# Keeping the residual in the output: accumulating stores, layer-norm sums by transfer, and a lead-in in 256-token blocks

## The chip, the cores and the metric

The kernel runs on one core of a Trainium2 chip. Its engines are TensorE (PE in the profile, its weight loads PEld), VectorE (DVE), ScalarE (ACT), GpSimd (POOL) and SyncE (SP), which here only issues transfers. The metric is the device time of one execution in microseconds; lower is better. Before the change it is 1020.83 us, the median of 3 runs (1020.34 to 1025.84).

## The reference, cut to what matters

Two batches of 1024 tokens with 2048 features. A quantized product with a context matrix is added to x, then a linear layer with a routed low-rank term is added to that:

```python
q1 = fake_quant(layernorm(x), x1_scale, x1_zp)      # (2, 1024, 2048)
q2 = fake_quant(ctx, x2_scale, x2_zp)               # (2, 2048, 2048)
x2 = x + q1 @ q2
xf = layernorm(x2)
probs = softmax(xf @ W_router.T)                    # 8 experts, the best 2, renormalized to w
h = einsum('td,erd->ter', xf, lora_A)               # rank 16
lora = einsum('ter,eor,te->to', h, lora_B, w) * 2
out = x2 + xf @ W_base.T + b_base + lora
```

## The kernel before, in words

Everything is held transposed, features on partitions and tokens along the row. An output row is 128 features by 1024 tokens of float32, 512 KB; there are NT = 16 of them in each of NB = 2 batches.

First product. A batch of x is loaded in 8 tiles of 128 tokens (`xn_load`), VectorE takes statistics (L333), GpSimd five tiny steps (L336 to L340), ScalarE quantizes to bytes (L348), TensorE transposes the bytes (L361), and VectorE or ScalarE writes them back as bf16 (L376, L378). A context row is loaded, quantized (L400) and converted to bf16 by VectorE, ScalarE or GpSimd (`ctx_conv`, L410 and L412). `gemm1` (L455) multiplies it into two PSUM banks; `evac1` (L473) scales the sum and adds x. That is an output row of x2. `keep` stores it to the DRAM tensor `kept`. Rows of batch 0 stay in SBUF (`XA`), those of batch 1 pass through two stage buffers.

In the lead-in the first three output rows are made together, while the tiles of batch 0 come in: the first 512 tokens of each row, then 256, then 256.

Layer norm over x2. The sum over the 16 rows is gathered row by row (`add0`, `add1`, L508), a matmul with a constant spreads the mean (`ones`, L485), VectorE subtracts it (`centre0` L520, `centre1` L549), ScalarE squares (L526, L556), and VectorE or GpSimd sum the squares (`square0` L533; `centre1` L557). `var_a` (L569 to L578) and `var_b` turn the sum into the scale. For batch 1 the rows are read back from `kept` (`tile_load`), and the centred ones go through DRAM and come back (`ln_load`).

Second product. The 2048 by 2048 matrix product of a batch is done as 8 blocks of 256 features. A block takes 7 products instead of 8, from sums and differences of quarters of the operand (`y_operands`, L616 to L618) and of the weights (`w_sum` L810), each value split in two f16 halves: the high half on ScalarE (`w_hi` L826), the low one as a difference on VectorE or GpSimd (`w_lo` L831, with `la`, `lt`, `lb` in `y_operands` at L617). `product` (L865 to L867) and `tail` (low-rank term, L886 to L888) fill three of six PSUM banks; the next block uses the other three. A weight scale is found by `w_norm`, with one small step on GpSimd (L709). `lora_h` is at L968 to L970.

Around the change. For each block, `ob_load` brings two output rows of `kept` back into a buffer, `ob_bias` (L905, ScalarE) adds the bias, and `post` adds scaled PSUM banks to the buffer (L915, VectorE, six times a block), apart from product 0, which is copied to a second bank (L929 ScalarE, L931 VectorE). `store` writes the buffer to the output. TensorE waits for some of these evacuations: product 3 for that of product 0, product 4 for that of 2, product 5 for that of 1, product 6 for that of 4.

Each engine has its own queue (`Line`), served strictly in order, with semaphore waits ahead of each instruction. The order is made by a plan: `at(t, f, ...)` gives each step a planned time, steps are sorted by it, and the table `V` holds offsets and the choice of engine ("a", "d", "p" for ScalarE, VectorE, GpSimd). SyncE's transfers (`Loads`) are sorted by the same times. The planned times only fix an order. A slow path for other zero points is skipped: each engine loads a flag (set by VectorE, L240) and branches, before the first instruction of the planned work (`both`, L1298; L1296 loads the flag).

Of the kernel before, what the change touches and what calls it, by code (L numbers as in the profile page):

```python
# [4 lines left out]
ACT = mybir.ActivationFunctionType  # L5
# [11 lines left out]
NT = 16  # L17
# [8 lines left out]
    "ctx_load": (-21.4, -16.79), "x_load": (-8.52, -2.7), "ctx_quant": (-10.38, -11.98), "ctx_conv": (-8.14, -5.53),  # L26
    "quant_on": "aaaaaaaaaaaaaaaaaaaaaaaaaaaaaaaa", "conv_on": "ddpappdpapaapdaadaadaaaaaapapdap", "evac_a": (9.81, 3.95),
    "evac_b": (5.43, 6.35), "keep": (20.76, 3.77), "ln1_step": 10.32, "xn_load": -13.2, "ln1_stats": -2.38,
    "ln1_quant": 3.24, "ln1_turn": 13.26, "ln1_back": 15.39, "back_on": "dddaaadd", "add0": 9.92, "mean": 3.5,
    "centre": 2.69, "centre_step": 2.3, "square": 2.58, "square_on": "dpppdppppppdpppd", "add1": 8.92, "sq_end": 6.2,  # L30
    "var_a": 7.58, "var_b": 12.06, "early": (8.48, 4.32, 10.86, 17.6, 0.72, 14.76, -4.36), "ops0": -54.07,
    "ops0_step": 9.0, "ops0_in": (3.06, 3.83, 1.69, 0.31, 2.05, -0.86, 3.32, 3.28), "lt_on": "pdpppdpddddddddd",
    "add1_on": "ppdddpddpppppppd", "sq1_on": "pdpppdpdppdddpdp", "lb_on": "dddddddddddddddd", "y_on": "ad",
    "post": ((-0.42, -0.62, 0.55, 0.9, 4.11, 0.34, 0.76), (1.78, 2.26, 0.1, 1.17, 1.58, 0.41, 1.32)),
    "la_on": "dpdddpdddpdpdpdp", "first_raw": -11.49, "first_ring": -0.52, "raw0": 8.82, "norm1": 40.01,
    "norm1_step": 6.14, "tile_load": -5.9, "cd_store": 1.64, "yd_store": 1.76, "var1": 7.44, "ops1": 11.14,
    "ops1_step": 19.58, "ln_load": 2.27, "ops1_in": (10.61, 1.45, 3.66, 2.38, 5.98, 7.8, 9.35, 3.61), "start": 32.08,
    "pair": 39.04, "a_load": 8.72, "a_prep": 18.75,
    "router": ((3.6, -4.9, 12.48, 1.98, 4.87, 8.83, 9.75, 24.24, 22.77), (1.64, -15.29, 12.16, 0.96, 2.87, 21.06, 13.87, 14.95, 23.73)),
    "w_load": (-31.54, -27.81, -27.96, -19.33), "b_load": -27.3,  # L40
    "w_norm": ((-20.87, -23.36, -22.49, -22.9), (-14.88, -21.6, -16.62, -15.26)),
    "w_scaled": ((-16.21, -11.48, -15.49, -9.58), (-12.98, -14.22, -14.22, -2.35), (-22.26, -18.56, -24.17, -27.91), (-18.78, -10.27, -4.7, -8.89)),
    "w_b": (11.13, -5.59, -17.37, -1.76),
    "w_op": ((-11.4, -3.44, -3.15, -9.51, -7.61, 8.03, 4.96), (-10.2, -7.05, 0.4, -4.29, 5.17, 2.6, 1.94), (-13.14, 16.12, 2.8, -20.29, 13.81, 2.35, 14.01), (6.02, -16.16, 16.7, 8.23, -0.09, 12.25, -1.78)),
    "w_sum": (8.38, 1.9, 0.3, -25.41, 1.16, 1.16, -3.26), "lo_on": ("pdpddpp", "pdppddp"), "ob_load": (-6.91, -12.75),
    "ob_bias": (-0.26, 1.49),
# [3 lines left out]
class Line:  # L50
# [6 lines left out]
    def do(self, waits, emit):  # L57
        self.work.append((waits, emit))
        self.done += 1
        return (self.sem, self.done)  # L60

    def run(self, eng, first=0, last=None):
        for waits, emit in self.work[first:last]:
# [46 lines left out]
def xattn_lora_ffn(nc, xn, xT, cT, qp, wT, bias, aT, rT, bT, outT, kept, maps):  # L110
# [107 lines left out]
    sl_yl = slots("sl_yl", 7)  # L218
# [322 lines left out]
    def tile_load(i):  # L541
        s = i % 2
        tile_in[i] = sp.do(tile_free[s] + [keep_out[NT + i]], sl_tb[s], tb[s], kept[1, i])
        tile_free[s] = None
# [826 lines left out]
```

## Time and profile before

| | |
|---|---|
| time, median of 3 runs | 1020.83 us (1020.34 to 1025.84) |
| the profiled execution | 1021.56 us, of which its span is 1018.8 us |
| mean granted clock of TensorE | 0.983 of full speed |
| busy: PE, DVE, ACT, POOL | 939.1, 631.1, 505.3, 303.2 us |
| moved by transfers | 211.74 MB, mean 208 GB/s |

The span runs from the first to the last instruction; the rest of the execution's own time lies around it. Busy time counts instructions that compute, not waits and not the issuing of transfers. A name such as "DVE S L810" is the engine, the tile written and the line of the kernel. A group of instructions shows busy time, the mean duration in ns and the idle time ahead with what ended it.

### The profile page before, as it was taken

How to read it: one execution, taken by the hardware profiler on the slowest of the kernel's cores; microseconds unless marked ns; L12 is line 12 of the kernel's file. 1: busy time of each engine (PE TensorE's matmuls, PEld its weight loads, DVE VectorE, ACT ScalarE, POOL GpSimd, SP SyncE). 2: the span in 40 equal slices, each digit the busy share in tenths (PEclk: the TensorE clock that was granted, in tenths of full speed). 3: DMA queues.
4: the chain of work that ended last, by engine and by line, in shares of the span. 5: the costliest groups of instructions: out<-in, count | busy, mean ns of one | idle time of the engine just before them, and what ended most of it. 6: DMA issues, size and time to landing. Idle time of an engine off the chain costs nothing. (4 is left out here: it accounts for less than half of the span.)

```text
span 1018.8 us, 12800 instructions
## 1 busy us (share of the span) xinstructions
PE 939.1 (92%) x4448; PEld 433.8 (43%) x4470; DVE 631.1 (62%) x760; ACT 505.3 (50%) x473; POOL 303.2 (30%) x217
## 2 busy tenths in 40 slices
PE   1899999998778898999899899998999999999998
PEld 0454444443334444344344344443444444444443
DVE  5788677989988585757869787315643253252251
ACT  4765676965556465555556565304443333334330
POOL 3333204836532053333314222102122122121220
PEclk9999999999999899999999999999999999999999
DMA  9789996876630557756675685991332332322311
GB/s 349 313 325 399 394 334 247 292 262 209 256 140 22 212 199 254 257 210 225 213 263 194 217 285 181 363 397 67 124 141 77 124 123 95 124 103 114 125 42 41
DMA packets 65044, 211.74 MB, mean 208 GB/s; under 512 B 6096, under 2 KB 22608, under 8 KB 56400
## 3 DMA queue, kind: packets, MB, share of 16 engines
q1 hardware_dynamic: 64976, 210.86, 56.5%
q8 instruction: 39, 0.64, 0.2%
q14 instruction: 29, 0.24, 0.1%
HBM read 154.22 MB, written 56.62 MB: 207 GB/s over the span
## 5 line engine op out<-in xcount | busy, mean ns | idle before, releaser
L831 POOL TENSOR_TENSOR Q<-S,Q 128x1024 f16<-128x1024 f32 x43 | 95.3, 2223 | 228.0 <-ACT Q L826 202.3
L826 ACT ACTIVATE Q<-S 128x1024 f16<-128x1024 f32 x74 | 77.2, 1049 | 114.5 <-DVE S L810 113.6
L867 PE MATMUL PS<-XA,Q 128*128 128x512 f16 x336 | 127.3, 379 | 0.0
L865 PE MATMUL PS<-XA,Q 128*128 128x512 f16 x336 | 127.3, 379 | 0.0
L866 PE MATMUL PS<-XA,Q 128*128 128x512 f16 x336 | 127.3, 379 | 0.0
L455 PE MATMUL PS<-Q,S 128*128 128x512 bf16 x501 | 114.5, 386 | 13.3 <-POOL S L412 6.0
L793 ACT ACTIVATE S<-S,WC 128x1024 f32<-128x1024 f32 x64 | 70.1, 1139 | 98.9 <-DMA S<-in_wT_dram 70.3
L455 PE MATMUL PS<-EX,S 128*128 128x512 bf16 (+1 forms) x502 | 106.4, 369 | 4.8 <-DVE st L333 2.0
L915 DVE SCALAR_TENSOR_TENSOR Q<-PS,WC,Q 128x512 f32<-128x512 f32 x72 | 53.6, 747 | 90.2 <-PE PS L888 60.7
L865 PE MATMUL PS<-EX,Q 128*128 128x512 f16 x256 | 98.6, 385 | 11.7 <-DVE S L915 7.1
L867 PE MATMUL PS<-EX,Q 128*128 128x512 f16 x256 | 98.5, 385 | 0.0
L866 PE MATMUL PS<-EX,Q 128*128 128x512 f16 x256 | 98.3, 384 | 0.0
L810 DVE TENSOR_TENSOR S<-S 128x1024 f32<-128x1024 f32 x64 | 93.7, 1466 | 5.2 <-ACT S L793 3.9
L831 POOL TENSOR_TENSOR S<-S 128x1024 f16<-128x1024 f32 x21 | 46.8, 2231 | 162.1 <-ACT S L826 156.8
L455 PEld LDWEIGHTS PS<-Q,S 128*128 128x128 bf16 x512 | 50.4, 100 | 76.6 <-POOL S L412 6.7
L455 PEld LDWEIGHTS PS<-EX,S 128*128 128x128 bf16 x512 | 50.2, 99 | 57.4 <-DVE EX L378 3.7
L915 DVE SCALAR_TENSOR_TENSOR S<-PS,WC,S 128x512 f32<-128x512 f32 x24 | 17.9, 745 | 83.0 <-PE PS L888 82.8
L865 PE MATMUL PS<-XA,S 128*128 128x512 f16 x176 | 66.7, 379 | 0.0
L867 PE MATMUL PS<-XA,S 128*128 128x512 f16 x176 | 66.7, 379 | 0.0
L866 PE MATMUL PS<-XA,S 128*128 128x512 f16 x176 | 66.7, 379 | 0.0
L826 ACT ACTIVATE S<-S 128x1024 f16<-128x1024 f32 x38 | 39.6, 1048 | 54.1 <-DVE S L810 54.0
L400 ACT ACTIVATE S<-S,cst 128x2048 uint8<-128x2048 f32 x30 | 62.5, 2082 | 4.5 <-DMA S<-in_cT_dram 4.5
(217 smaller groups left out, 1617.9 us busy)
## 6 DMA issues: line engine op xcount, KB each, us to landing
S<-in_cT_dram SPq DMA_DIRECT2D x32, 1024.0 KB, 8.0
S<-in_wT_dram SPq DMA_DIRECT2D x32, 1024.0 KB, 5.4
EX<-in_xn_dram SPq DMA_DIRECT2D x24, 512.0 KB, 7.5
Q<-kept_dram SPq DMA_DIRECT2D x24, 512.0 KB, 6.5
S<-kept_dram SPq DMA_DIRECT2D x24, 512.0 KB, 4.6
out_dram<-Q SPq DMA_DIRECT2D x24, 512.0 KB, 2.9
yops_dram<-S SPq DMA_DIRECT2D x48, 256.0 KB, 3.3
XA<-in_xT_dram SPq DMA_DIRECT2D x16, 512.0 KB, 9.0
```

Of the source, the lines that this page charges most:

```text
L400: f = lambda e: e.activation(u8b[u], ctx_f[s], ACT.Identity, bias=z2, scale=inv2)
L455: ins = e.matmul(bank(a)[:, t0 % 512:t0 % 512 + t1 - t0], q2[q][:, 128 * k:128 * (k + 1)], q1T[b][:, k, t0:t1], start=(k == 0), stop=(k == ...
L793: scaled_w[i, q] = [act.do([raw_in[q // 2]] + w_scale[i % 8][0], lambda e, v=v: e.activation(v, v, ACT.Copy, bias=0.0, scale=c[:, 4:5]))]
L810: sub = lambda w, dst, x, y, op=ALU.subtract: [dve.do(w, lambda e: e.tensor_tensor(dst, x, y, op))]
L826: tok["hi", n] = s, free, src, act.do(w + free, lambda e: e.activation(ring[s][:, 0:1024], src, ACT.Copy, bias=0.0, scale=1.0))
L831: l = line.do([h] + free, lambda e: e.tensor_tensor(ring[s][:, 1024:2048], src, ring[s][:, 0:1024], ALU.subtract))
L865: e.matmul(bank(bk), wh[:, c], yh(op, k), start=(fresh and k == 0), stop=False, skip_group_check=not fresh)
L866: e.matmul(bank(bk), wh[:, c], yl(op, k), start=False, stop=False, skip_group_check=not fresh)
L867: ins = e.matmul(bank(bk), wl[:, c], yh(op, k), start=False, stop=(read and k == 7), skip_group_check=not fresh)
L915: ob_ready[i, h] = [dve.do(done + ob_ready[i, h] + w_scale[i % 8][2], lambda e: e.scalar_tensor_tensor(dst, src, kk, dst, op0=ALU.mult, op ...
```

## The change

1. `kept` is no longer used: `keep` stores rows of x2 into the output tensor, and what read `kept` reads the output.
2. For all blocks but the last, `ob_load` and `ob_bias` go. The first evacuation into each half of a buffer writes bias + scaled product (`first`, on ScalarE or VectorE by `first_on`; batch 0: one VectorE, three ScalarE; batch 1: four VectorE), and `store` becomes a transfer issued by GpSimd that adds the buffer to the output. The last block works as before, but stores each 128 x 512 quarter by itself once finished.
3. Six additions of layer-norm sums ("m" in `add1_on` at 9, 14, 15; in `sq1_on` at 1, 3, 15) become accumulating transfers from SBUF to SBUF issued by GpSimd. The "m" in `square_on` at 1 is at a place that isn't used.
4. The lead-in's products run in blocks of 256 tokens, in an order of their own, and VectorE's branch moves behind the statistics of the first two tiles. The lead-in's engines and times come from `V`.
5. `centre0` also waits for the row's `keep`. SyncE's last waits include the `keep` and last stores.
6. Most numbers in `V` and many engine choices are new, among them: conversions of context rows 1 and 2 on GpSimd, of the last row (31) on ScalarE (was GpSimd); the bank copy of batch 1 on ScalarE (was VectorE).

```diff
+    def move(self, waits, slot, dst, src):
+        self.work.append((waits, lambda e: e.dma_start(dst, src, accum_op=ALU.add), slot.sem))
+        return slot.next()
...
-            emit(eng).then_inc(self.sem, 1)
+            if moved is None:
+                emit(eng).then_inc(self.sem, 1)
+            else:
+                emit(eng).then_inc(moved, 16)
...
-        keep_out[g] = sp.do(w + both_halves(g), sl_keep[g % 4], kept[g // NT, g % NT], xt(g))
+        keep_out[g] = sp.do(w + both_halves(g), sl_keep[g % 4], outT[g // NT, g % NT], xt(g))
...
+    def add_to(on, w, acc, v, slot=sl_add):
+        if on == "m":
+            return pool.move(w, slot, acc, v)
+        return lines[on].do(w, lambda e: e.tensor_tensor(acc, acc, v, ALU.add))
...
+        def first(h, dst, src, on):
+            col = bo[:, 2 * (i % 8) + h:2 * (i % 8) + h + 1]
+            w = done + ob_free[(2 * i + h) % 4] + w_scale[i % 8][2] + [once["bo"]]
+            if on == "a":
+                e = act.do(w, lambda e: e.activation(dst, src, ACT.Identity, bias=col, scale=kk))
+            else:
+                e = dve.do(w, lambda e: e.tensor_scalar(dst, src, kk, col, op0=ALU.mult, op1=ALU.add))
...
-        elif n in (1, 4):
-            e = acc(1, L[:, t1], bank(bk))
...
+            e = acc(h, v, bank(bk)) if n in (4, 5) or i == LAST else first(h, v, bank(bk), V["first_on"][i // 8][{1: 0, 2: 1, 3: 2, 6: 3}[n]])
+            if i == LAST and n > 2:
+                last_store(h, 1 if n in (4, 5) else 0, v, e)
...
-        ob_free[d] = [sp.do(ob_ready[i, h], sl_out[d], outT[b, o], ob[d])]
+        ob_free[d] = [pool.move(ob_ready[i, h] + [keep_out[NT * b + o]], sl_out[d], outT[b, o], ob[d])]
...
+    at(V["l_stats"][1] + 0.01, split_dve)
...
+    for n, (g, t0, t1) in enumerate(((0, 0, 256), (1, 0, 256), (0, 256, 512), (1, 256, 512), (2, 0, 256), (2, 256, 512),
+                                     (0, 512, 768), (1, 512, 768), (2, 512, 768), (0, 768, 1024), (1, 768, 1024), (2, 768, 1024))):
+        at(V["l_gemm"][n], gemm1, g, t0, t1, 0, 16)
```

## Rows read from the trace of the kernel before

**Rows 1.** The page: span, and TensorE's busy time.
```profile
span 1018.8 us, 12800 instructions
...
PE 939.1 (92%) x4448; PEld 433.8 (43%) x4470; DVE 631.1 (62%) x760; ACT 505.3 (50%) x473; POOL 303.2 (30%) x217
```

**Rows 2.** Busy time by stretches: length, then engines as named, clock, DMA share, GB/s.
```profile
0.00:60.00 60.00, 31.95 (x187) 20.21 (x191) 42.58 (x70) 35.83 (x20) 19.07 (x54) 1.00 0.83 317
...
150.00:350.00 200.00, 173.79 (x821) 78.69 (x830) 165.95 (x202) 125.82 (x117) 91.40 (x41) 0.96 0.58 208
...
400.00:650.00 250.00, 232.69 (x1054) 104.56 (x1053) 184.06 (x214) 143.28 (x161) 80.49 (x39) 0.97 0.66 234
...
750.00:1019.00 269.00, 264.89 (x1228) 119.84 (x1226) 95.56 (x100) 87.23 (x87) 53.58 (x25) 1.00 0.26 101
```

**Rows 3.** Waits of TensorE in 400 to 650 (total, times, longest); its timeline.
```profile
PE PS L865 <- DVE S L915: 11.1, 3, 4.1
...
496.15 0.38 PE L865 MATMUL PS<-EX,Q 128*128 128x512 f16 x1 [4.14 <-DVE S L915]
```

**Rows 4.** Timelines of VectorE and GpSimd: start, us, instruction, idle time ahead.
```profile
488.81 1.22 DVE L616 TENSOR_TENSOR S<-S,PS 128x1024 f32<-128x1024 f32 x1 [1.06 <-DMA S<-centred_dram]
...
492.19 3.15 DVE L810 TENSOR_TENSOR S<-S 128x1024 f32<-128x1024 f32 x1
...
492.14 2.12 POOL L831 TENSOR_TENSOR S<-S 128x1024 f16<-128x1024 f32 x1 [6.42 <-ACT S L826]
...
535.99 1.22 DVE L810 TENSOR_TENSOR S<-S 128x1024 f32<-128x1024 f32 x1
```

**Rows 5.** Groups by shape, whole span: busy us, mean ns, idle before.
```profile
L915 DVE SCALAR_TENSOR_TENSOR Q<-PS,WC,Q 128x512 f32<-128x512 f32 x72 | 53.6, 747 | 90.2 <-PE PS L888 60.7 <-PE PS L867 28.0
...
L905 ACT ACTIVATE Q<-Q,bo 128x1024 f32<-128x1024 f32 x24 | 27.0, 1134 | 0.0
...
L929 ACT ACTIVATE PS<-PS 128x512 f32<-128x512 f32 x8 | 4.6, 580 | 0.0
```

**Rows 6.** Waits in 400 to 650 of SyncE's queue and of GpSimd.
```profile
SPq L102 <- DVE Q L915: 64.3, 14, 12.7
...
POOL Q L831 <- ACT Q L826: 59.4, 12, 6.5
```

**Rows 7.** The page's DMA issues: count, KB each, median us to landing.
```profile
out_dram<-Q SPq DMA_DIRECT2D x24, 512.0 KB, 2.9
...
kept_dram<-XA SPq DMA_DIRECT2D x16, 512.0 KB, 9.1
```

**Rows 8.** Timelines around the last output row of the first product, and low-rank product.
```profile
275.47 8.37 PE L455 MATMUL PS<-Q,S 128*128 128x512 bf16 x31 [6.02 <-POOL S L412]
...
270.59 2.96 POOL L617 TENSOR_TENSOR EX<-S,EX 128x1024 f16<-128x1024 f32 x1 [5.12 <-DVE PS L617]
...
262.22 2.08 ACT L400 ACTIVATE S<-S,cst 128x2048 uint8<-128x2048 f32 x1
...
311.05 0.38 PE L968 MATMUL PS<-XA,S 128*128 128x512 f16 x1 [1.53 <-DVE XA L617]
```

**Rows 9.** Timelines: last addition of batch 1's squares, and the variance's matmul.
```profile
449.46 2.37 POOL L557 TENSOR_TENSOR S<-S 128x1024 f32<-128x1024 f32 x1 [4.79 <-ACT S L556]
...
454.63 1.84 PE L569 MATMUL PS<-mean_w,S 128*128 128x1 f32 x16
```

**Rows 10.** VectorE's first work, and the first four half tiles, issue to landing.
```profile
3.07 0.16 DVE L240 TENSOR_TENSOR flag<-rr 128x1 int32<-128x1 f32 x1
9.72 2.47 DVE L333 BATCH_NORM_STATS2 st<-EX 128x6 f32<-128x512 f32 x4 [6.49 <-issue]
...
L102 SPq DMA_DIRECT2D EX<-in_xn_dram x4: 420/432/432, 1.2 to 2.6; - x4
...
DMA to landing us min/median/max: 4.2/5.8/8.9
```

**Rows 11.** Timeline of SyncE: the last store's issue.
```profile
1015.71 0.33 SPq L102 DMA_DIRECT2D out_dram<-S  x1
```

More of the change, by code:

```diff
@@ L57, in do @@
     def do(self, waits, emit):
-        self.work.append((waits, emit))
+        self.work.append((waits, emit, None))
         self.done += 1
         return (self.sem, self.done)
+    def move(self, waits, slot, dst, src):
+        self.work.append((waits, lambda e: e.dma_start(dst, src, accum_op=ALU.add), slot.sem))
+        return slot.next()
     def run(self, eng, first=0, last=None):
-        for waits, emit in self.work[first:last]:
+        for waits, emit, moved in self.work[first:last]:
             for sem, value in waits:
                 eng.wait_ge(sem, value)
-            emit(eng).then_inc(self.sem, 1)
+            if moved is None:
+                emit(eng).then_inc(self.sem, 1)
+            else:
+                emit(eng).then_inc(moved, 16)
 class Slot:
@@ L507, in add1 @@
         else:
-            sums[1] = [lines[V["add1_on"][nt]].do(sums[1] + both_halves(NT + nt), lambda e: e.tensor_tensor(acc1, acc1, t, ALU.add))]
+            sums[1] = [add_to(V["add1_on"][nt], sums[1] + both_halves(NT + nt), acc1, t)]
         stage_free[nt % 2] = stage_free[nt % 2] + sums[1]
@@ L556, in centre1 @@
             sq = act.do([y] + sq_free[s], lambda e: e.activation(sq1[s], v, ACT.Square))
-            sums[1] = [lines[V["sq1_on"][i]].do(sums[1] + [sq], lambda e: e.tensor_tensor(acc1, acc1, sq1[s], ALU.add))]
+            sums[1] = [add_to(V["sq1_on"][i], sums[1] + [sq], acc1, sq1[s])]
             sq_free[s] = list(sums[1])
@@ L1106, in split_here, with split_dve @@
         sp.split = len(sp.work)
+    def split_dve():
+        assert sorted(front) == [(0, 0), (0, 1)]
+        dve.split = len(dve.work)
     P = Plan()
@@ L1275, in xattn_lora_ffn @@
         for h in range(2):
-            at(us(t + V["ob_load"][h]), ob_load, i, h)
-            at(us(t + V["ob_bias"][h]), ob_bias, i, h)
+            if i == LAST:
+                at(us(t + V["ob_load"][h]), ob_load, i, h)
+                at(us(t + V["ob_bias"][h]), ob_bias, i, h)
+            else:
+                at(us(t + V["store"][h]), store, i, h)
         when = [5.12 * n for n in range(6)] + [33.3]
@@ L1312, in _ @@
             sp.run(eng, sp.split, None, case)
-            for s in sl_out:
+            for s in sl_keep + sl_out + sl_last:
                 eng.wait_ge(s.sem, 16 * s.n)
```

105 lines of the change are left out of this document (53 added, 52 removed).

## The prediction

> **What bounds the kernel now.** First the page's busy shares: TensorE is busy for 939.1 of 1018.8 us [rows 1], so I ask where the other 80 us are and which engine makes them. The table by stretches [rows 2] answers: 28.0 us idle in 0 to 60 (the lead-in), 26.2 in 150 to 350 (first layer norm of the output, operands of batch 0, low-rank term), 17.3 in 400 to 650 (blocks of batch 0 with the second layer norm beside them) and 4.1 behind 750, nearly all of it the tail. The column PEclk adds the time that TensorE ran at the lower of its two levels, 1.2 GHz instead of 2.4: 0.97 over 250 us is 7.5 us of lost work, 0.96 over 200 us is 8. What a change can win lies in three places, then: about 28, 34 and 25 us. From 750 to the tail TensorE never waits and nothing can be won.
>
> Next, who ends these waits. In 400 to 650 it is VectorE's evacuation L915: 11.1 us in three waits, the longest 4.14 us [rows 3]. That one, read on VectorE and GpSimd, is a queue and not one slow instruction [rows 4]: the subtraction L616 waits 1.06 us for a reloaded centred row, a sum L810 takes 3.15 us instead of the 1.22 of its neighbour because a GpSimd subtraction that began 0.05 us earlier runs for 2.12 us, and only then comes the L915 on which TensorE waits. So this stage is bound by the length of VectorE's queue.
>
> **Part 1: the residual stays in the output.** In each of the 16 blocks but the last, two loads of 512 KB, two ScalarE bias additions of 1.134 us and the read-modify-write form of four of the six evacuations go. In batch 0 three of the four become ScalarE activations (0.58 us by the nearest row, the copy L929) and one stays on VectorE. VectorE loses 3 x 0.747 = 2.2 us a block, 18 us over eight blocks; ScalarE loses 2 x 1.134 and gains 3 x 0.58, so 0.5 us less [rows 5]. In batch 1 VectorE sheds eight bank copies, where TensorE has no idle time: worth nothing.
>
> The stores leave SyncE's queue. Today they hold it: 64.3 us in 14 waits in 400 to 650 alone [rows 6], with the loads of weights and centred rows behind them. They go to GpSimd's queue, which is busy 80 of 250 us there, as 30 accumulating transfers, and the weights' low halves (L831) and the small step L709 then stand behind them. GpSimd now comes to an L831 5.0 us before its input is there (59.4 us over 12 waits) [rows 6]. The stores are placed at 33.0 and 42.7 us of a block whose last evacuations come at about 32.6 and 38.5, so they should find their rows ready.
>
> No row shows an accumulating transfer or one issued by GpSimd. For the landing, the nearest rows are 512 KB in 2.9 us (store) and in 9.1 us (store under load) [rows 7]; a buffer is wanted again two blocks, some 78 us, later, so either hides. For GpSimd's own time I take 1 us, near SyncE's 0.33 us an issue [rows 11], with 0.33 and 9.1 as ends. Even 9.1 fits the idle share (2 x 9.1 in a block of 39 us), but a subtraction queued behind it comes late; that is the fourth case below. The Trainium skill (DMA: Bandwidth & Descriptors, section "Anatomy of one DMA") gives 2.0 us plus bytes over 436 GB/s for such a transfer, 3.2 us here as an estimate; nothing here shows it, and the sum below would be 1 us lower by it, since the wait of part 3 would vanish.
>
> What this wins: of the 4.14 us stall, 1.06 (the reload, queued behind stores) and 0.75 (an evacuation ahead) go by rows 4 and 5, that is 1.8 or 44%. The GpSimd overlap stays, and the evacuation that TensorE waits for there is a read-modify-write that stays on VectorE. I apply a third, not 44%, to the stage's 25 us, because every instruction's place is re-planned and new meetings will form: **-8 us**, ends -25 (all of it) and +8 (as much lost as I count won).
>
> **Part 2: layer-norm sums by transfer and new placing, 60 to 350.** Three adds of the batch-1 sum leave GpSimd (2) and VectorE (1). The largest stall of this stage is 6.02 us before the last output row of the first product: its conversion sat on GpSimd, in order behind a subtraction that ended at 273.55, though its quantized input was ready on ScalarE at 264.30 [rows 8]. That conversion is now ScalarE's, so this stall goes, 6.0 us, with 1.7 for one stretch at the lower clock. But most is given back at once: what TensorE does next ends on operands that VectorE makes without a pause, and it waited for them at 311.05. There VectorE sheds one add (1.2) and one low-half subtraction (1.2); the earlier product does not speed that chain. I take **-3 us**, ends -7.7 (nothing given back) and +5 (four conversions more on VectorE in the first half of the rows, 1.2 us each, should they land in its full stretch).
>
> **Part 3: the last add of the batch-1 squares** becomes a transfer and gates the variance's matmul. Now it starts at 449.46 and takes 2.37 us on GpSimd; the matmul comes at 454.63 with no wait [rows 9]. With a landing of 2.9 to 9.1 us the sum is there at 452.4 to 458.6, so the wait is 0 to 3.9 us: **+1 us**. The same kind of step earlier in the chain has 6 us between rows and hides.
>
> **Part 4: lead-in.** VectorE takes the general-case branch behind two tiles' statistics and no longer ahead of them. Now it sets the flag at 3.07 and starts statistics only at 9.72, 6.5 us idle, while the first half tile had landed at 1.2 + 4.2 = 5.4 and, by the median of the four, the second near 7 [rows 10]. If the branch costs little when taken later, 9.7 - 5.4 = 4.3 us are won. If it costs its 6.5 us again: tile 1's last half lands at 2.6 + 8.9 = 11.5, its statistics end near 13.0, and VectorE is back at 19.5 with 5.4 us of work done (two tiles of four statistics, 2.47 us, and their aggregation), where today it has done 9.8 by then. That is 4.4 late, less two passes of 1.2 us net that leave it, so 2.0 late. Blocks of 256 tokens let TensorE begin with tiles 0 and 1 alone, but the conversion of the first context row now stands behind tiles 2 and 3 on VectorE, so it begins no sooner, and the last tile comes at about the same time either way. I take **0**, between ends of -4.3 and +2 and nearer the second: three microseconds of the idle time lie behind the landings, so the branch itself is dear.
>
> **Tail.** Last store issued 1015.71, span end 1018.8 [rows 11, 1]: 3.1 us for 512 KB. It becomes quarters of 256 KB: **-0.3**, ends 0 and -1.5.
>
> **Sum.** 0 - 8 - 3 + 1 - 0.3 = -10.3. The profiled execution took 1021.56 us for a span of 1018.8, so 1011.3 for one like it; that execution lies 0.73 above the median of 1020.83, so 1010.5. I say **1011**.
>
> **Rivals.**
> *Everything in 400 to 650 goes.* 184 us of VectorE work in 250 leave room, and 13 go. Against it: the GpSimd overlap that made half of the long stall is untouched. -25 - 3 - 0.3 + 1 gives 994; with half of the gain beyond mine, 1001.
> *Given back: no change.* GpSimd's issues hold the port or buffers that VectorE's two-input sums need, as its subtraction did for 1.93 us in rows 4. Sixteen issues in batch 0 at 1.93 us are 31 us of VectorE time at worst, 18 less what evacuations freed: the stage keeps its 25 us, and 1020.8 - 3 + 1 - 0.3 + 1.7 is 1020. For it: VectorE is 74% busy there. Against: no row says that an issue does what a 1024-wide subtraction does. The Trainium skill's page SBUF — State Buffer ("Who interferes with whom") has descriptor writes by GpSimd and VectorE's two-port modes exclude each other; by that rule it is the transfer that waits, and the trace shows the exclusion only between compute instructions.
> *Slower: the stores block GpSimd's queue.* Place: a store waits, or is being issued, while a low half (L831) for TensorE's next product stands behind it. It decides from the point where wait and issue together exceed the 5.0 us by which GpSimd is now ahead [rows 6]. Price: a stall like the longest now, 4.14 us, with 1.7 at the lower clock, once in three of the eight blocks of batch 0 is +17.5, and no gain of 8: 1020.8 - 2.3 + 17.5 = 1036. For it: in-order queues did just this with the 6.02 us conversion. Against: GpSimd idles two thirds of that stage.
>
> **How the numbers follow.** Forecast (1003 to 1016) 0.48, no change 0.23, slower 0.20, far faster 0.09. A measurement here can tell 0.5%, about 5 us. So faster (under 1015.7) 0.56, the same 0.23, slower (over 1025.9) 0.21. The range of the forecast alone is 1003 to 1017; to hold 8 in 10 it must take in no change and the nearer part of the slower case: **999 to 1031**.
>
> **What would show it.** Right: in the table by stretches the idle time and PEclk of 400 to 650 improve to some 17 us together; no wait over 4 us for L915; no wait near the last output row of the first product, but a longer one for VectorE's operands behind it; SyncE no longer waits for L915. Part 4: a gap of about 6 us on VectorE behind tile 1. Wrong: waits of TensorE for GpSimd's L831, GpSimd waiting for L915 with L831 behind it, VectorE sums of 2 us or more beside issues, or a new wait over 4 us at the variance matmul.

## The result, and the profile after

| | before | changed |
|---|---|---|
| median (range, executions) | 1021.43 us (1019.02 to 1025.84, 20) | 1018.19 us (1010.24 to 1022.36, 20) |
| ratio, 95% interval | | 0.9963 [0.9946, 0.998] |
| measured again beside experiments | 1021.26; 1021.95 us | 1014.45, ratio 0.993 [0.9912, 0.9948]; 1016.51, ratio 0.9956 [0.9936, 0.9976] |

The forecast was 1011, a gain of 10. The first measurement gives a gain of 3.2 us; the three ratios average 0.995, a gain of 5 us: right in direction and inside the range, but half the size or less. The changed kernel's executions spread over 12 us where those of before spread over 7, so below I also compare stages of the profiled executions. The repeats are e5 (1014.45) and e15 (1016.51). Of e5 I had expected 1016 to 1019 if the kernel itself varies and some 1012 if the first chip was unlucky; it came between.

The changed kernel's profiled execution took 1018.26 us. Its page: span and busy times, the DMA queues (packets, MB, share of 16 engines' span) and GpSimd's stores (KB each, us to landing).

```profile
span 1016.5 us, 12911 instructions
...
PE 938.8 (92%) x4518; PEld 438.7 (43%) x4518; DVE 613.5 (60%) x708; ACT 495.4 (49%) x475; POOL 357.3 (35%) x267
...
q1 hardware_dynamic: 56624, 179.40, 48.6%
q0 software_dynamic: 5184, 18.88, 11.1%
...
out_dram<-Q POOLq DMA_DIRECT2D x23, 512.0 KB, 5.5
```

VectorE does 17.6 us less and GpSimd 54.1 more than in [rows 1], of which 31.7 are its 36 issues (of GpSimd, unlike SyncE, the page counts issues as busy time). The new queue q0 is GpSimd's: 18.88 MB in 11.1% of the transfer engines' time, where q1 moves 9.5 times as much in 4.4 times the time. That disproportion is the key to this case. (5.5 us is the landing of the 23 stores from buffers called Q; the seven from buffers called S took 7.9.) Next the table by stretches, columns as in [rows 2]:

```profile
0.00:60.00 60.00, 31.56 (x236) 25.32 (x237) 37.98 (x62) 37.71 (x21) 15.85 (x50) 1.00 0.85 319
...
150.00:350.00 200.00, 177.86 (x837) 79.87 (x835) 161.36 (x194) 120.96 (x111) 93.78 (x45) 0.94 0.60 208
...
400.00:650.00 250.00, 228.99 (x1047) 103.38 (x1046) 171.37 (x194) 144.04 (x166) 92.19 (x52) 0.98 0.67 202
...
750.00:1017.00 267.00, 263.09 (x1219) 119.11 (x1217) 102.39 (x79) 77.95 (x82) 93.22 (x51) 1.00 0.32 84
```

In 400 to 650 VectorE lost 12.7 of its 184.1 us of work, as forecast, and yet TensorE's idle time did not fall: 21.0 us here, 18.2 and 17.1 in the profiles of e5 and e15, against 17.3 before. The waits of that stretch, of TensorE, VectorE, GpSimd and SyncE, say where to look; they answer to [rows 3, 6]:

```profile
POOL Q L854 <- ACT Q L849: 60.8, 12, 11.5
...
DVE S L639 <- DMA S<-centred_dram: 20.3, 11, 3.4
...
PE PS L888 <- DVE S L938: 10.4, 3, 5.4
```
```profile
SPq L117 <- ACT S L641: 71.4, 24, 10.0
SPq L115 <- DMA centred_dram<-S: 32.4, 6, 9.0
```

The same two waits in the kernel before, VectorE's for the reload and SyncE's for the landing of a centred row that it has stored:

```profile
DVE S L616 <- DMA S<-centred_dram: 3.4, 4, 1.1
```
```profile
SPq L100 <- DMA centred_dram<-S: 20.1, 5, 9.7
```

(L639, L854, L888, L938 and L641 were L616, L831, L865, L915 and L618 before.) VectorE waits 20.3 us for reloaded centred rows, six times as long as before (15.2 and 14.4 in e5 and e15). SyncE no longer waits for evacuations, as forecast, but it is held as long by the next step in its order: the operand quarters of L641, 71.4 us (66.9 and 68.8 in e5 and e15) against the 64.3 for L915, and by the centred rows' own stores, 32.4 us against 20.1. One stall read on VectorE, then on TensorE:

```profile
577.10 2.43 DVE L639 TENSOR_TENSOR S<-S,PS 128x1024 f32<-128x1024 f32 x2 [3.40 <-DMA S<-centred_dram]
579.63 1.42 DVE L640 TENSOR_TENSOR S<-S 128x512 f32<-128x512 f32 x2
580.97 1.22 DVE L833 TENSOR_TENSOR S<-S 128x1024 f32<-128x1024 f32 x1
582.10 0.74 DVE L938 SCALAR_TENSOR_TENSOR S<-PS,WC,S 128x512 f32<-128x512 f32 x1
```
```profile
583.00 0.58 PE L888 MATMUL PS<-EX,S 128*128 128x512 f16 x1 [3.87 <-DVE S L938]
```

This is the queue of [rows 4] again, with 3.40 us of waiting at its head instead of 1.06. TensorE's wait (3.87) is about that wait plus a short step, so by these rows, though no run shows it for this one stall, the evacuation would have come nearly in time without it.

I cut the execution at TensorE's last low-rank product (`tail`) of block 0 and of block 7. "Reload wait" is VectorE's for `centred_dram` in 400 to 650.

| kernel (profiled execution, us) | to block 0 | blocks 1 to 7 | rest | reload wait |
|---|---|---|---|---|
| before | 369.4 | 301.6 | 347.8 | 3.4 |
| changed, three profiles (first, e5, e15) | 369.3, 368.9, 369.3 | 303.2, 301.7, 300.8 | 344.0, 344.0, 345.6 | 20.3, 15.2, 14.4 |
| forecast of the difference | -3 | -8 +1 | -0.3 | |

So blocks 1 to 7 won nothing, the way to block 0 won nothing, and what was won in the profiles lies behind block 7, where I had said next to nothing could be. Of the kernel before there is one profile only. The kernel of e7 (below), which differs from it in the lead-in alone, took 371.5, 303.1 and 346.2 us: differences of up to 2 us between single profiles can be chance.

### The profile page after: what moved, and what is told of

Read it like the earlier page. It is cut to its first block, busy times and chain, and to the rows that moved or that the text cites. A ratio compares the mean times of both kernels' runs of the same rounds, so it can differ in the third digit from the quotient of the medians.

```text
span 1016.5 us, 12911 instructions
## 1 busy us (share of the span) xinstructions
PE 938.8 (92%) x4518; PEld 438.7 (43%) x4518; DVE 613.5 (60%) x708; ACT 495.4 (49%) x475; POOL 357.3 (35%) x267
## 3 DMA queue, kind: packets, MB, share of 16 engines
q0 software_dynamic: 5184, 18.88, 11.1%
## 4 chain that ended last, share of the span: by engine, by line
PE 46%; DVE 9%; DMA 9%; issue 4%; ACT 2%; POOL 2%; SPq 0%; DVEq 0%; ACTq 0%; POOLq 0%
PE PS L888 13%; PE PS L890 12%; PE PS L889 12%; DMA S<-centred_dram 4%; DVE S L640 4%; DMA yops_dram<-S 2%; DMA S<-in_wT_dram 2%; DVE S L639 1%; PE PS L1002 1%; PE PS L1003 1%; PE PS L1004 1%; PE PS L909 1%; PE PS L911 1%; PE PS L910 1%; PE PS L1045 1%
## 5 line engine op out<-in xcount | busy, mean ns | idle before, releaser
L854 POOL TENSOR_TENSOR Q<-S,Q 128x1024 f16<-128x1024 f32 x54 | 117.8, 2189 | 124.3 <-ACT Q L849 118.1
L888 PE MATMUL PS<-XA,Q 128*128 128x512 f16 x336 | 127.3, 379 | 1.3 <-POOL Q L854 1.3
L833 DVE TENSOR_TENSOR S<-S 128x1024 f32<-128x1024 f32 x64 | 102.0, 1594 | 33.2 <-POOL Q L854 20.9
L472 PE MATMUL PS<-Q,S 128*128 128x512 bf16 x512 | 116.7, 390 | 5.3 <-POOL S L429 3.0
L888 PE MATMUL PS<-EX,Q 128*128 128x512 f16 x256 | 98.5, 385 | 13.5 <-DVE S L938 6.5
L854 POOL TENSOR_TENSOR S<-S 128x1024 f16<-128x1024 f32 x26 | 58.9, 2270 | 56.2 <-ACT S L849 56.2
L472 PEld LDWEIGHTS PS<-EX,S 128*128 128x128 bf16 x544 | 53.8, 99 | 50.6 <-DVE st L350 0.9
L523 POOL TENSOR_TENSOR S<-S 128x1024 f32<-128x1024 f32 x25 | 63.0, 2529 | 26.9 <-ACT S L549 13.2
L71 POOL DMA_DIRECT2D out_dram<-Q x23 | 20.2, 879 | 140.8 <-DVE Q L947 105.9
L888 PE MATMUL PS<-XA,S 128*128 128x512 f16 x176 | 66.7, 379 | 0.0
L640 DVE TENSOR_TENSOR S<-S 128x512 f32<-128x512 f32 (+2 forms) x68 | 64.5, 969 | 2.3
```

Source lines behind the costliest of these rows:

```text
L71: self.work.append((waits, lambda e: e.dma_start(dst, src, accum_op=ALU.add), slot.sem))
L472: ins = e.matmul(bank(a)[:, t0 % 512:t0 % 512 + t1 - t0], q2[q][:, 128 * k:128 * (k + 1)], q1T[b][:, k, t0:t1], start=(k == 0), stop=(k == ...
L523: return lines[on].do(w, lambda e: e.tensor_tensor(acc, acc, v, ALU.add))
L640: diff = lambda dst, x, y, w, line=dve: line.do(w, lambda e: e.tensor_tensor(dst, x, y, ALU.subtract))
L833: sub = lambda w, dst, x, y, op=ALU.subtract: [dve.do(w, lambda e: e.tensor_tensor(dst, x, y, op))]
L854: l = line.do([h] + free, lambda e: e.tensor_tensor(ring[s][:, 1024:2048], src, ring[s][:, 0:1024], ALU.subtract))
```

## Experiments

**One, two and no accumulating packets.** In 400 to 650 q0 of the changed kernel moved 6.80 MB in 16.1% of 16 x 250 us, which is 388 ns for each 4 KB on one engine. The first run (e3) makes GpSimd's 30 stores plain, which leaves the residual out of all blocks but the last. The six sums by transfer still accumulate.

```diff
-        ob_free[d] = [pool.move(ob_ready[i, h] + [keep_out[NT * b + o]], sl_out[d], outT[b, o], ob[d])]
+        pool.work.append((ob_ready[i, h] + [keep_out[NT * b + o]], lambda e: e.dma_start(outT[b, o], ob[d]), sl_out[d].sem))
+        ob_free[d] = [sl_out[d].next()]
```

> The changed kernel, whose 30 stores by GpSimd are plain and not accumulating (the residual is left out of all but the last block of the output). Theory A: nothing that TensorE waits for changes, 1016 to 1020, VectorE's waits for the reload stay near 20 us. Rival B: the operands' stores land in 3.3 us again and not 4.0, the waits halve and the time is 1010 to 1013.

It took 1012.48 us (ratio 0.9921 [0.9894, 0.9947]) and the reload wait was 8.1 us: the rival's time and its halved wait, though the operands' stores landed in 3.7 us and not in 3.3. Since the changed kernel's own measurements differed by 3.7 us, this was repeated on one chip with the changed kernel and with two that store each buffer twice, the second time into the scratch tensor:

```diff
+        ob_free[d].append(pool.move([], sl_dup[d], kept[b, o], ob[d]))
```

In the second of them (e14) the additional transfer is plain:

```diff
+        pool.work.append(([], lambda e: e.dma_start(kept[b, o], ob[d]), sl_dup[d].sem))
+        ob_free[d].append(sl_dup[d].next())
```

> The changed kernel, and behind each of GpSimd's 30 accumulating stores a second one of the same buffer into the scratch tensor, so the accumulating packets are doubled (16 more of 512 KB in batch 0, 14 in batch 1); its output is the same. Theory (packets of 389 ns hold the transfer engines, the reload of centred rows comes late, VectorE's evacuation with it): 4 to 8 us over the changed kernel beside it, waits for the reload in 400 to 650 of 25 us or more (20.3 and 15.2 in the two profiles of the changed kernel), and 2 us or more above the next kernel. Rival (the packets are hidden and the lost microseconds are the new order's): within 2 us of the changed kernel beside it.

> The changed kernel, and behind each of GpSimd's 30 accumulating stores a second, plain one of the same buffer into the scratch tensor: the same additional issues on GpSimd (0.88 us each) and the same bytes from SBUF, but packets of 181 ns by the plain stores seen so far. Theory (the time of the packets is the price): 1 to 4 us over the changed kernel and 2 us or more below the kernel with doubled accumulating stores. Rival 1 (GpSimd's issue is the price): the same as that kernel within 1 us. Rival 2 (hidden): within 1 us of the changed kernel.

> The changed kernel as it is, on the chip of the two runs with doubled stores, since its own two measurements (1018.19 and 1014.45 us) differ by more than the effect in question. Theory: 1014 to 1018, below both of the others. Rival (hidden): the three lie within 2 us.

> The changed kernel with GpSimd's stores as plain transfers, residual left out of all blocks but the last (1012.48 us when run beside a changed kernel of another job), now on the chip of the changed kernel and of the doubled stores, so that none, one and two accumulating packets of each row stand on one scale. Theory: 3 to 6 us under the changed kernel beside it, and as far below it as the doubled one lies above. Rival (hidden): within 2 us of it.

| stores of each row | median us | ratio | blocks 1 to 7 | reload wait |
|---|---|---|---|---|
| plain (e16) | 1011.58 | 0.9914 [0.9882, 0.9946] | 297.2 | 7.4 |
| accumulating, as changed (e15) | 1016.51 | 0.9956 [0.9936, 0.9976] | 300.8 | 14.4 |
| accumulating and plain (e14) | 1029.08 | 1.0073 [1.0044, 1.0103] | 308.6 | 21.1 |
| accumulating twice (e13) | 1046.38 | 1.0254 [1.022, 1.0288] | 325.9 | 26.9 |

Queue q0 on the page and the stretch 400 to 650, first of the kernel with plain stores (e16):

```profile
q0 software_dynamic: 5184, 18.88, 5.6%
```
```profile
400.00:650.00 250.00, 235.98 (x1074) 106.60 (x1073) 175.21 (x194) 143.98 (x165) 88.61 (x52) 0.97 0.62 217
```

then of the one that stores accumulating and plain (e14):

```profile
q0 software_dynamic: 9504, 34.61, 14.6%
```
```profile
400.00:650.00 250.00, 229.03 (x1025) 102.07 (x1024) 166.53 (x198) 141.23 (x162) 92.90 (x61) 0.96 0.69 220
```

and of the one that accumulates twice (e13):

```profile
q0 software_dynamic: 9504, 34.61, 19.0%
```
```profile
400.00:650.00 250.00, 219.31 (x964) 96.84 (x961) 157.96 (x189) 132.74 (x152) 88.24 (x56) 0.93 0.72 210
```

The same 18.88 MB take 11.1% when all 36 transfers accumulate and 5.6% when only the six sums do, and TensorE's idle time in the stretch is 14.0 us with plain stores against 21.0 in the first profile of the changed kernel, 18.2 in e5's and 17.1 (250 - 232.94) in the one of the same chip.

The trace also shows whom the packets delay. SyncE's stores of centred rows landed in 3.8 us (median of 16) in the kernel before, 5.1 to 5.3 in the three profiles of the changed kernel, and 4.6 with plain stores; SyncE's wait for them in 400 to 650 was 20.1, 31.4 to 32.4 and 23.3 us. Of the reloads behind operand stores in that stretch, the second half of each pair landed in 4.8 us before (mean of seven, at most 5.7), in 5.1 to 6.0 in the changed kernel (at most 6.2 to 8.6), and in 4.6 to 4.8 with plain stores (at most 5.4).

The two doubled kernels issue the same number of transfers and bytes and lie 17 us apart. That is the price of the accumulating packets together with that of GpSimd's issues, which differ too: the additional ones took 1.18 us each in e13 and 0.83 in e14, not 0.88 as I had assumed. No wait of TensorE between blocks 0 and 7 ends with GpSimd in either, so the packets are the likelier part, but these runs don't separate the two. The cost isn't linear: removing the first accumulating packet of a row gives back 4.9 us (0.42% of 1021.95, give or take 0.38, so just clear of nothing; blocks 1 to 7 below say the same), a second one costs 29.9; the rival "hidden" falls, and e13's forecast of 4 to 8 was far too small, e14's of 1 to 4 as well. Part of e13's price is the clock: its 400 to 650 has 13.6 us more idle time of TensorE than e15's and a granted clock of 0.93 against 0.97, which is another 10 us. The additional issue with plain packets alone cost 12.6 us; how much of that is GpSimd's issue time and how much the bytes, these runs don't tell. And some of it is no effect of the stores at all: the profiled executions of e13 and e14, the slowest of each, reach the end of block 0 at 373.4 and 373.0 us where e15's does at 369.3, and the first additional store is issued at 369.

In blocks 1 to 7 the three plain variants lie at 296.6 (e3), 297.2 (e16) and 296.5 (e10, below), eight accumulating ones in the new order at 297.9 to 303.9. The 297.9 is e1's, next; the other seven took 300.8 or more.

**When the reload is asked for.** The new plan stores the operand quarters 7.08 us behind their step, where it was 1.76, and SyncE reloads centred rows behind these stores: the last of them and the reload were issued 2.5 to 3.8 us apart before and 2.5 to 4.4 after (seven reloads in 400 to 650). One number is put back (e1):

```diff
+V['yd_store'] = 1.76
```

> One number of the changed kernel is put back: the stores of the second batch's operands stand 1.76 us behind their step in SyncE's order, as before the change, and not 7.08. Theory A (the reload of the centred rows is late because the re-planned order stores the operands, and so frees their buffers, later): VectorE's waits for the reload in 400 to 650 fall from 20.3 us to under 8, TensorE's idle time there from 21 us to about 12, and the time from 1018.2 to about 1010. Rival B (the accumulating transfers slow the plain ones, so the reload is late wherever its stores stand): the waits stay at 15 us or more and the time within 3 us of 1018.

1015.16 us (ratio 0.9949 [0.9923, 0.9974]), reload wait 13.8 us: the time lies between the changed kernel's own measurements, so no gain is shown, and theory A's 1010 and under 8 us of waiting were missed. Blocks 1 to 7 took 297.9 us in its profile, nearly as little as with plain stores and with twice their reload wait; e6 and e11 below, with the same edit, took 301.2 and 301.7, so I take that for chance, but no run repeats it. The second run (e11), on the kernel with both this edit and the branch first, asks for the reload 6 us ahead of its step:

```diff
-        at(us(u - V["ln_load"]), ln_load, k)
+        at(us(u - (V["ln_load"] if k == 0 else 6)), ln_load, k)
```

> The version with VectorE's branch first and the operand stores early, with the reload of centred rows 1 to 15 planned 6 us ahead of the step that reads them, where it was 0.42. Theory (the subtraction on VectorE waits for the reload because it is asked for too late, behind slow accumulating packets): the waits for it in 400 to 650, 11.3 us there, fall under 5, TensorE's idle time in that stretch falls by 2 to 4 us, time 1007 to 1010. Rival (the transfer engines are what is short, so an earlier request only moves the queue, and SyncE then waits longer for the row's own store and holds weights): waits of 8 or more, 1010 to 1015.

1012.79 us (ratio 0.991 [0.9883, 0.9936]) with 15.6 us of waiting, against 1011.34 and 11.3 of the kernel that it is made from (e6, below). The rival held: an earlier place in SyncE's order brings nothing. SyncE waited 67.9 us for L642 (the changed kernel's L641) and 31.2 for the row's own store, where it had 66.6 and 31.5: it is held in both by the same two steps, and in SyncE's order a reload still stands behind the operand stores of the step ahead of it.

**The branch and the 256-token blocks.** The line that moves the branch goes (e4):

```diff
-    at(V["l_stats"][1] + 0.01, split_dve)
```

> The changed kernel with VectorE's branch back ahead of all statistics; the lead-in still runs in 256-token blocks. My account (the branch costs 6 us of VectorE wherever it stands): the fourth output row starts at 56 to 58 us as now (57.4), time 1017 to 1019. Rival (the moved branch wins what lies ahead of the data): the fourth row starts 2 to 4 us later and the time is 1020 to 1022.

1010.32 us (ratio 0.99 [0.9868, 0.9932]), better than both my account (1017 to 1019) and the rival (1020 to 1022); the profiled execution was its slowest, 1018.88. VectorE in the changed kernel, then in this one:

```profile
5.68 2.58 DVE L350 BATCH_NORM_STATS2 st<-EX 128x6 f32<-128x512 f32 x4 [2.32 <-DMA EX<-in_xn_dram]
...
12.52 0.26 DVE L351 BATCH_NORM_AGGREGATE mv<-st 128x2 f32<-128x24 f32 x1
18.84 2.47 DVE L350 BATCH_NORM_STATS2 st<-XA 128x6 f32<-128x512 f32 x4 [6.06 <-issue]
```
```profile
9.70 2.48 DVE L350 BATCH_NORM_STATS2 st<-EX 128x6 f32<-128x512 f32 x4 [6.44 <-issue]
12.21 0.26 DVE L351 BATCH_NORM_AGGREGATE mv<-st 128x2 f32<-128x24 f32 x1
12.39 2.41 DVE L350 BATCH_NORM_STATS2 st<-EX 128x6 f32<-128x512 f32 x4
14.83 0.26 DVE L351 BATCH_NORM_AGGREGATE mv<-st 128x2 f32<-128x24 f32 x1
15.01 2.41 DVE L350 BATCH_NORM_STATS2 st<-XA 128x6 f32<-128x512 f32 x4
```

The branch costs 6.06 us in one place and 6.44 in the other. Taken early, it lies beside the loads, and four tiles' statistics then follow without a gap: tile 2's begin at 15.0 instead of 18.8. The fourth output row begins at 53.76 us instead of 57.43 (the bounds of the lead-in):

```profile
57.43 0.81 PE L472 MATMUL PS<-EX,S 128*128 128x512 bf16 x3
```
```profile
53.76 1.46 PE L472 MATMUL PS<-EX,S 128*128 128x512 bf16 x6
```

So moving the branch costs TensorE 3.7 us at its fourth row. That this is also what it costs in time is likely and not shown as exactly: no changed kernel ran beside e4, and on the chip of e5 (1014.45) the kernel with branch first and operand stores early took 3.1 us less (e6). The changed lead-in in the kernel before, branch moved too (e7):

```diff
+    at(V["l_stats"][1] + 0.01, split_dve)
...
+    for n, (g, t0, t1) in enumerate(((0, 0, 256), (1, 0, 256), (0, 256, 512), ...)):
+        at(V["l_gemm"][n], gemm1, g, t0, t1, 0, 16)
```

> The kernel before with only the changed lead-in (256-token blocks, its times and engines, VectorE's branch behind two tiles' statistics). Theory: the moved branch costs what the blocks win and a little more, so TensorE starts the fourth output row at 57.5 to 59 us and the time is 1020 to 1024. Rival: the lead-in is what the change wins, 1016 to 1018.

1019.32 us (ratio 0.9978 [0.9962, 0.9994]), fourth output row at 57.74, reload wait 4.1: the lead-in as changed brings TensorE no sooner to its fourth row, and the 0.2% has no place that I can name.

**Structure against order.** The changed structure (residual in the output, 256-token lead-in) with the kernel before's table of times and engines, first accumulating (e2), then plain (e12, residual left out):

```diff
+V['ctx_load'] = (-21.4, -16.79)
...
+V['yd_store'] = 1.76
...
+V['store'] = (33.5, 40.0)
```

> The changed structure (residual in the output, accumulating stores by GpSimd, 256-token lead-in) with the planned times and engine choices of the kernel before wherever that had one, so without accumulating transfers for layer-norm sums. Theory A (structure is good, new order costs what it wins): the stage 400 to 650 has about 10 us idle, VectorE's waits for the reload under 8 us, time 1011 to 1015; the 6.0 us stall ahead of the last output row is back. Rival B (accumulating transfers slow the others): idle time of that stage 20 us or more, time 1018 to 1026.

> The changed structure in the order and with the engine choices of the kernel before (1024.59 us with accumulating stores), now with plain stores by GpSimd: the residual x2 is left out of all blocks but the last. Theory (the old order loses in part because accumulating packets delay the reload its order was not made for): 1018 to 1020, waits for the reload in 400 to 650 under 8 us (14.2 with accumulation), the wait for an evacuation near 632 (5.99 us) shorter by 2 or more. Rival (the old order loses because the changed steps meet at new places in VectorE's queue, whatever the packets take): 1023 to 1026, with the waits near 544 and 632 still above 4 us.

1024.59 us (ratio 1.0039 [1.0013, 1.0065]) and 1023.75 (1.0029 [1.0009, 1.0049]). In the old order the structure loses, and the packets aren't shown to be the cause: e2 came in the rival's range, but with plain stores the time is the same within the intervals, though the reload wait falls from 14.2 to 6.8 us, and the two long waits for an evacuation stay.

```profile
539.15 0.59 PE L956 MATMUL PS<-EX,S 128*128 128x512 f16 x1 [5.01 <-DVE Q L1006]
...
627.33 0.59 PE L956 MATMUL PS<-EX,Q 128*128 128x512 f16 x1 [5.27 <-DVE Q L1006]
```

e12's rival held. The opposite mix (e8) keeps the new order but gives batch 0 its old structure back, stores, loads, bias additions and evacuations alike (branch first here too; of the edit two places are shown, the first line shortened):

```diff
+            e = acc(h, v, bank(bk)) if n in (4, 5) or i == LAST or i < 8 else first(...)
...
+        if i < 8:
+            ob_free[d] = [sp.do(ob_ready[i, h], sl_plain[d], outT[b, o], ob[d])]
```

> Branch first, and the blocks of batch 0 take the residual as before (row loaded, bias added on ScalarE, six read-modify-write evacuations on VectorE, plain store by SyncE), while batch 1 keeps the accumulating stores. Theory (accumulating packets take twice the time of plain ones on the transfer engines and make the reload late, which costs more than the evacuations win): VectorE's waits for the reload fall under 10 us, time 1005 to 1009. Rival (VectorE's relief by the new evacuations carries the gain): 1012 to 1020, with waits of TensorE for L915's counterpart longer.

1034.37 us (ratio 1.0133 [1.0109, 1.0157]), far outside the theory (1005 to 1009) and the rival (1012 to 1020). Its waits of TensorE and SyncE in 400 to 650:

```profile
PE PS L889 <- ACT S L791: 17.4, 2, 9.2
```
```profile
SPq L117 <- DVE Q L939: 87.7, 11, 15.1
```

SyncE stands 87.7 us behind evacuations, and VectorE's reload wait is 19.2 us (up to 6.9), though no store accumulates there and the reloads themselves landed in 3.6 and 4.4 us: a late request alone makes the reload late. TensorE's two long waits end with L791, the squares of a raw weight on ScalarE, whose queue had itself stood 7.6 us for the subtraction behind the reload (at 515, ahead of the wait that ends at 524). So the new order doesn't work with batch 0 as it was. That it is the stores in SyncE's queue that break it is my reading: e8 put back loads, bias additions and evacuations with them.

**Toward a better one.** Branch first and operand stores early (e6):

> Branch ahead of all statistics and operands' stores at 1.76 us, the two single undoings together. If their gains are separate places (lead-in; reload in the blocks of batch 0) they add: 1007 to 1009. If both only shift where a low-clock stretch falls, the sum is no better than one of them: 1010 to 1013.

1011.34 us (0.9904 [0.9884, 0.9924]), no different from the branch alone. On it, the six sum additions on engines again (e9; five where they were, that of the second square on GpSimd and not on VectorE), and, by itself, plain stores (e10):

```diff
+V['add1_on'] = 'ppdddpddpppppppd'
+V['sq1_on'] = 'ppppddpdpppdpddp'
```

> The version with VectorE's branch first and the operand stores 1.76 us behind their step (1011.34 us when last run), and in it the six additions of layer-norm sums go back from accumulating transfers to GpSimd and VectorE. Theory (these six transfers were worth nothing, since the chain they left was not what TensorE waited for; they hold the transfer engines as the stores do, but are only 3 MB): 1010 to 1013, the same as before within 0.3%. Rival (they took work off full engines, 2.4 us of GpSimd or 1.2 of VectorE each, five of them beside TensorE's stalls in 250 to 460): 1014 to 1018, with longer waits of TensorE in 250 to 460.

> The version with VectorE's branch first and the operand stores early, with GpSimd's 30 stores as plain transfers: the residual x2 is left out of all blocks but the last. Theory (the accumulating packets, 389 ns against 186, delay the reload of centred rows, and that costs what the change does not win): 5 to 7 us less than with accumulation, so 1004 to 1006, waits for the reload in 400 to 650 under 8 us. Rival (with the operand stores early the reload is no longer held up by the stores, so the price of accumulation is hidden): 1009 to 1012.

Without the sum transfers 1018.07 us (0.9973 [0.9955, 0.999]), as the rival had it: the theory that they are worth nothing fell. Its low-rank product begins 4.2 us later than that of e6; both on TensorE:

```profile
289.12 0.59 PE L1005 MATMUL PS<-XA,S 128*128 128x512 f16 x1 [8.72 <-DVE S L778]
```
```profile
284.92 0.59 PE L1003 MATMUL PS<-XA,S 128*128 128x512 f16 x1 [6.99 <-ACT Q L867]
```

Block 0 ends at 372.3 instead of 364.5, of which some 6 us are the granted clock (0.93 against 0.96 in 150 to 350), so the place of the loss is less certain than its size between the medians. With plain stores 1008.49 us (0.989 [0.9861, 0.9919]), some 3 below e6, within the intervals of both; the theory's 1004 to 1006 was missed, though blocks 1 to 7 took 296.5 us and the reload wait was 7.6. Of the kernels that compute everything, the three that are the change with the branch first (e4, e6, e11) are the fastest (1010.3 to 1012.8): 0.9 to 1.0% below the kernel before, where the change as made is 0.4 to 0.7% below.

## Why the prediction was half right

**Part 1, -8: this step failed.** Measured is +0.3 (mean of three, 301.9 against 301.6; the old structure's stage also gave 303.1 in e7). The failed term is the wait for the reload: the prediction let "1.06 (the reload, queued behind stores)" go. It grew to 3.40, and in all from 3.4 us to 14.4 to 20.3: (a) SyncE freed of the output stores waits as long for operand quarters, and the reload stands behind those; (b) the accumulating packets hold the transfer engines twice as long. I had asked what a landing of 9.1 us does to the *buffer*, and answered "hides", which was right; I did not ask whom the packets delay on the engines that all queues share. By the plain variants (b) is worth 5 us (301.9 against a mean of 296.9 in e3 and e16; 3.6 for the two that ran on one chip); in it are also the 0.3 us by which GpSimd issues a plain store faster. With plain stores the stage wins 4.7 of the 8. The other 3.3 stay open: (a) is argued, from the wait of 71.4 us, the 7 to 8 us of reload wait that plain stores leave, and e8, but e1 and e11, which moved steps in SyncE's order, won nothing back; and the 8 itself was a third of the stage's loss that I took without a row. Of Part 1's smaller steps, as predicted or nearly so: GpSimd's issue was 0.88 us where I took 1, the rows were ready, GpSimd is still ahead of L854 (60.8 us over 12 waits, 5.1 each), and first evacuations took 0.76 us on ScalarE where I took 0.58. The Trainium skill (DMA: Bandwidth & Descriptors, "Anatomy of one DMA") gave 3.2 us as an estimate for such a store's landing; plain ones by GpSimd landed in 3.0 (median of 23; 4.2 to 4.6 for the other seven) and accumulating ones in 5.5 (7.9), so it fits the former alone.

(In the first rival, "half of the gain beyond mine" is 1002 and not 1001; nothing hangs on it.)

**Rival "given back": near in its time, wrong in its mechanism.** Its 1020 is 2 us from the first measurement and 4 to 6 from the others. It had GpSimd's issues slow VectorE's sums, 16 times in batch 0. Of the 1024-wide sums that began during an issue, the three with no GpSimd subtraction behind it took 1.22 us as ever; seven, with one right behind, took 3.96, all in batch 1, where TensorE waits for nothing. In 400 to 650 no such sum began during an issue, so the rival's price was never met there, and that is the order's luck and not a rule. What is shown to be given back there went through the transfer engines. **Rival "stores block GpSimd's queue"** did not occur: in 400 to 650 GpSimd stood at a store for no more than 0.8 us at a time, with 0.88 for the issue far from the 5.0, and no wait of TensorE there ends with GpSimd. In batch 1 it did stand at stores, 105.9 us in six waits for L947, but there TensorE waited for nothing.

**Part 2, -3: measured -0.2 at the end of block 0.** The 6.02 us stall went, as forecast:

```profile
264.37 8.77 PE L472 MATMUL PS<-Q,S 128*128 128x512 bf16 x32 [3.05 <-POOL S L429]
...
287.17 0.59 PE L1002 MATMUL PS<-XA,S 128*128 128x512 f16 x1 [6.63 <-ACT Q L865]
```

but half of it came back one row earlier, again behind a GpSimd subtraction (an L640 of 2.96 us ahead of the conversion), and the first product ended 3.3 us sooner only for TensorE to wait 6.63 for the next operands. I had named this chain and given it 4.7 of the 7.7; it took all. The 1.7 for the clock, part of those 7.7, came and went by execution: the granted clock of 150 to 350 was 0.94 here, 0.97 in e5 and e15, and 0.96 before. That the sum transfers are worth more than one addition's time, e9 shows by its median; that it is here, one profile says, at another clock.

**Part 3, +1: did not come.** The changed kernel's profile has no wait at the variance's matmul, e5's one of 0.3 us; that is inside the bounds (0 to 3.9).

**Part 4, 0: right, with its mechanism** (57.43 against 57.24; the 6 us gap behind tile 1). What I missed is that the two halves cancel: e4 shows the rest of the new lead-in (blocks of 256 tokens, its order and engines) worth some 3.5 us (53.76 against 57.24), and the branch's move costs them.

**Behind block 7, -0.3: measured -3.8, -3.8 and -2.2.** I wrote that VectorE's eight bank copies in batch 1 are worth nothing since TensorE has no idle time there. In its first block it had: a wait of 1.56 us at 713 with such a copy (L931) in VectorE's queue 0.8 us ahead. Here is the kernel before, then the changed one:

```profile
690.00:700.00 10.00, 7.73 (x86) 3.65 (x88) 3.44 (x4) 4.13 (x5) 2.13 (x1) 0.83 0.20 76
700.00:750.00 50.00, 48.44 (x242) 22.69 (x234) 32.57 (x47) 22.96 (x24) 12.86 (x6) 1.00 0.24 87
```
```profile
690.00:700.00 10.00, 7.73 (x94) 3.77 (x95) 2.44 (x4) 4.66 (x6) 2.99 (x2) 1.00 0.72 219
700.00:750.00 50.00, 50.00 (x246) 23.46 (x239) 34.38 (x45) 20.75 (x23) 18.74 (x11) 1.00 0.20 59
```

The wait is gone in all three profiles. It ends 0.84 us behind the start of that copy, after 1.56 to 1.58 us, in each of the four kernels with this copy on VectorE (before, e7, e2, e12), also in the two that have the new structure. The stretch at the lower clock behind the router's wait (clock 0.83 in 690 to 700, 1.7 us) is gone in two of three, in e15 it is back, and that one's rest is 345.6 and not 344.0; it is also gone in e7, where nothing behind the lead-in was changed, so these 1.7 us are luck. The last 0.5 is the tail.

**Sum by stage:** forecast -3 -7 -0.3; measured, as means of three profiles, -0.2 +0.3 -3.3, which is -3.2 between spans (1015.6 against 1018.8); the medians give 3.2, 6.8 and 5.4. The profiled executions of e5 and e15 lie 2.0 and 1.0 us above their medians, so the stages hold less of the gain than the medians; where the rest of it lies stays open.

## What to carry to other kernels

Transfers moved to another queue still share the transfer engines: cost their packets' time against the most urgent load of that stretch, not only the landing against their own buffer. A freed in-order queue stops at its next wait; look up which step that is before counting the gain. And when a large edit brings new structure and a new order at once, neither alone needs to help (here 1024.6 us for the structure in the old order and 1034.4 for the new order with batch 0's old structure, against 1018.2 together), so forecast their meeting, not their parts.

## What the runs showed of the hardware that was not expected

- An accumulating transfer took 388 ns for each 4 KB on a transfer engine (16.1% of 16 x 250 us for 6.80 MB), a plain one of the same queue 183 or less (7.6% for 6.82 MB in e16, where one of 13 transfers still accumulates). It landed in 5.5 us instead of 3.0, and GpSimd's issue took 0.88 us instead of 0.57. Over the whole span the packets of all 36 transfers come to a mean of 392 ns (11.1% for 4608 of 4 KB); with 30 transfers plain, 5.5% of the 16 engines' time less for their 3840 packets makes a plain one some 160 ns (an estimate from the shares).
- The price grew faster than the transfer engines' time: with them 62, 67, 69 and 72% busy in 400 to 650, blocks 1 to 7 took 297, 301, 309 and 326 us (the last two also issue twice as often on GpSimd). The Trainium skill (DMA: Bandwidth & Descriptors, "Queues, rings and completion order") has each engine take turns between its queues packet by packet. That long packets of one queue then delay the other's is my inference; SyncE's stores of centred rows, 4.6 us with plain and 5.3 with accumulating stores of GpSimd beside them, agree.
- A 1024-wide sum of VectorE that began while GpSimd issued a transfer, with a subtraction of GpSimd's following at once, took 3.95 to 3.97 us instead of 1.22, seven times of seven in each of the changed kernel's three profiles: it ended 1.1 us behind the subtraction, as if it had waited for that one. VectorE, then GpSimd, in the changed kernel:

```profile
749.21 3.96 DVE L833 TENSOR_TENSOR S<-S 128x1024 f32<-128x1024 f32 x1 [4.18 <-POOL Q L854]
```
```profile
749.06 0.87 POOL L71 DMA_DIRECT2D out_dram<-Q  x1
749.67 2.41 POOL L854 TENSOR_TENSOR Q<-S,Q 128x1024 f16<-128x1024 f32 x1
```

- VectorE's jump over the skipped path cost 6.06 to 6.49 us wherever it stood (6.49 in the kernel before). The Trainium skill (Runtime: NRT & Kernel Launch, "Instruction fetch mechanics") has a taken branch outside the fetched window wait for a fetch, without a figure. The gaps here fit that, but no row shows the fetch.
